# The search for the expert thresholds, its rounds written out and its reached values written turned

## The reference, cut to what matters

```python
def _L0_ffn_ref(x, gate_w, w1, w2):                 # x is (B=4, T=1024, C=256), after attention and layer norm
    cap = int(EXPERT_CAPACITY * T / E)              # E = 8 experts, cap = 256
    probs = jax.nn.softmax(jnp.einsum('BTC,CE->BTE', x, gate_w), axis=-1)
    top_p, top_idx = jax.lax.top_k(jnp.transpose(probs, (0, 2, 1)), cap)
    xin = jnp.take_along_axis(x[:, None, :, :], top_idx[..., None], axis=2)
    h = jax.nn.gelu(jnp.einsum('BElC,ECH->BElH', xin, w1), approximate=False)
    y = jnp.einsum('BElH,EHC->BElC', h, w2) * top_p[..., None]
    return jnp.zeros((B, T, C), x.dtype).at[b_idx, top_idx].add(y)
```

## Time and profile before

| what | value |
|---|---|
| median of 3 runs | 505.44 us (503.3 to 505.83) |
| the profiled execution | 505.29 us, span 503.6 us |
| PE busy | 460.6 us (91% of the span) |
| DVE busy | 309.9 us (62%) |
| ACT busy, POOL busy | 211.5 us, 189.0 us |
| the search (65.17 to 99.3 us of the span) | 34.1 us |
| mean granted TensorE clock | 0.941 of full |

### The profile page before, as it was taken

The page is one execution under the profiler, slowest core; times in us unless marked ns, Lnnn a source line. Parts: engine busy times, 40 slices in busy tenths (PEclk is TensorE's granted clock), DMA queues, the critical chain, the costliest instruction groups (busy, mean ns, idle before and its releaser), DMA issues.

```text
span 503.6 us, 9489 instructions
## 1 busy us (share of the span) xinstructions
PE 460.6 (91%) x3204; PEld 412.2 (82%) x3204; DVE 309.9 (62%) x825; ACT 211.5 (42%) x517; POOL 189.0 (38%) x175
## 2 busy tenths in 40 slices
PE   6999455568999999999999999999999999999992
PEld 5888344467999899989998999899989989999992
DVE  3787788877457545754665475557555664665450
ACT  1568498002244425524442354245424533452331
POOL 3322400051083518143722554174518252813332
PEclk9999655569999999999999999999999999999998
DMA  8963844023242615171517243433525171503131
GB/s 291 360 217 124 294 172 173 1 53 110 93 76 55 171 48 85 32 208 34 83 16 203 53 75 78 130 66 62 149 59 85 43 208 27 79 22 43 21 43 21
DMA packets 35666, 52.44 MB, mean 104 GB/s; under 512 B 3009, under 2 KB 28994, under 8 KB 35138
## 3 DMA queue, kind: packets, MB, share of 16 engines
q1 hardware_dynamic: 22400, 34.37, 20.5%
q0 software_dynamic: 12288, 17.08, 19.6%
q10 hardware_dynamic: 962, 0.80, 0.5%
HBM read 35.17 MB, written 16.92 MB: 103 GB/s over the span
## 4 chain that ended last, share of the span: by engine, by line
PE 77%; DVE 8%; issue 1%; POOL 1%; ACT 0%; DVEq 0%; POOLq 0%
PE wide L865 36%; PE bank L856 35%; PE bank L698 3%; DVE over L1124 2%; DVE floor L1137 1%; PE bank L831 1%; DVE cand L1119 1%; DVE reached L1131 1%; PE bank L815 1%; PE bank L902 1%; PE wide L698 1%; POOL out_dram L491 1%; PE bank L865 1%; DVE w1lo L1289 1%; DVE x_all L1024 0%
## 5 line engine op out<-in xcount | busy, mean ns | idle before, releaser
L865 PE MATMUL wide<-w2hi,hhi 128*128 128x256 f32 x504 | 145.4, 289 | 0.0
L491 POOL DMA_INDIRECT out_dram<-ysb,sidx x64 | 102.2, 1596 | 111.5 <-ACT ysb L651 95.1
L865 PE MATMUL wide<-w2hi,hlo 128*128 128x256 f32 x504 | 142.5, 283 | 0.0
L865 PE MATMUL wide<-w2lo,hhi 128*128 128x256 f32 x504 | 142.1, 282 | 0.0
L638 ACT ACTIVATE hraw<-bank 128x512 f32<-128x512 f32 (+1 forms) x136 | 77.6, 571 | 127.7 <-PE bank L856 124.6
L483 POOL DMA_INDIRECT xg<-xn_rows,gidx x64 | 65.2, 1018 | 156.8 <-issue 89.4
L1281 DVE CAST hhi<-hraw 128x512 fp32r<-128x512 f32 (+1 forms) x136 | 57.9, 426 | 86.9 <-ACT hraw L638 82.3
L865 PEld LDWEIGHTS wide<-w2hi,hhi 128*128 128x128 f32 x504 | 95.3, 189 | 3.7
L865 PEld LDWEIGHTS wide<-w2lo,hhi 128*128 128x128 f32 x504 | 95.1, 189 | 3.4
L865 PEld LDWEIGHTS wide<-w2hi,hlo 128*128 128x128 f32 x504 | 94.9, 188 | 0.0
L1283 DVE TENSOR_TENSOR hlo<-hraw,hhi 128x512 fp32r<-128x512 f32 (+1 forms) x136 | 90.4, 665 | 4.7
(11 more groups left out here) (175 smaller groups left out, 466.4 us busy)
## 6 DMA issues: line engine op xcount, KB each, us to landing
raw<-in_w_dram SPq DMA_DIRECT2D x16, 1024.0 KB
xn_rows<-x_all SPq DMA_DIRECT2D x4, 1060.0 KB, 4.0
raw<-in_x_turned_dram SPq DMA_DIRECT2D x8, 512.0 KB, 8.7
x_all<-in_x_dram SPq DMA_DIRECT2D x8, 512.0 KB, 9.7
out_dram<-x_all SPq DMA_DIRECT2D x8, 512.0 KB, 3.4
xg<-xn_rows,gidx POOLq DMA_INDIRECT x64
out_dram<-ysb,sidx POOLq DMA_INDIRECT x64
ctxT<-in_ctx_turned_dram ACTq DMA_DIRECT2D x1, 256.0 KB, 3.4
```

The source lines that it names most:

```text
L491: pool.indirect_dma_start(out=out_rows, out_offset=at, in_=ysb[g][:, i, :], in_offset=None, compute_op=ALU.add).then_inc(rows_added, 16)
L865: t = pe.matmul(y_tile(g, i, last), hh[s % 4][:, at:at + P], w[:, j, :], start=(j == 0 and m == 0 and (alone or i % 2 == 0)), stop=(j == H ...
```

## The change

The DVE loop over the rounds is gone: the four rounds that it held stand one after another, with the round as a constant. `reached` has the order batch, expert, bits: `keep_reached` writes each value 8 places (16 bytes) behind the one before, and `raise_floor` reads 8 in a row. `cand` and the counts have the order bits, batch, expert within a half, so `keep_reached` reads both in a row of 128; `compare` now reads `cand` in seven pieces of 8 that lie 16 values apart, and the matmul writes its 56 sums to seven pieces of 8 in PSUM.

```diff
-        cand = sb("cand", [P, B, KT + 1, E], I16)
+        cand = sb("cand", [P, 2, KT + 1, HB, E], I16)
...
-        reached = sb("reached", [P, B, KT + 1, E], I16)
+        reached = sb("reached", [P, B, E, KT + 1], I16)
...
-            return bank[h][:, 0:HB * (KT + 1) * E].rearrange("p (b n) -> p b n", b=HB)
+            return bank[h][:, 0:HB * (KT + 1) * E].rearrange("p (k b e) -> p k b e", b=HB, e=E)
...
-                            t = pe.matmul(counts(h)[:, b, E:], onesb[:], over[:, h * HB + b, c, :],
+                            t = pe.matmul(counts(h)[:, 1:, b], onesb[:], over[:, h * HB + b, c, :].rearrange("p (k e) -> p k e", e=E),
...
-                full = [P, HB, KT + 1, E]
-                dve.tensor_tensor(half(cand, h), half(floor_, h).unsqueeze(2).to_broadcast(full),
-                                  step_bits[:, bass.ds(r, 1)].to_broadcast(full), ALU.bitwise_or).then_inc(cand_ready[h], 1)
+                full = [P, KT + 1, HB, E]
+                steps = step_bits[:, r] if isinstance(r, int) else step_bits[:, bass.ds(r, 1)].rearrange("p r k e -> p (r k) e")
+                dve.tensor_tensor(cand[:, h], half(floor_, h).unsqueeze(1).to_broadcast(full),
+                                  steps.unsqueeze(2).to_broadcast(full), ALU.bitwise_or).then_inc(cand_ready[h], 1)
...
-                    half(cand, h)[:, b, 1:].unsqueeze(1).to_broadcast([P, TC, KT, E]), ALU.is_ge).then_inc(over_ready[h][b], 1)
+                    cand[:, h, 1:, b].unsqueeze(1).to_broadcast([P, TC, KT, E]), ALU.is_ge).then_inc(over_ready[h][b], 1)
...
-                dve.scalar_tensor_tensor(out=half(reached, h).rearrange("p b k e -> p b (k e)"), in0=counts(h),
-                                         scalar=float(CAP), in1=half(cand, h).rearrange("p b k e -> p b (k e)"),
+                dve.scalar_tensor_tensor(out=half(reached, h).rearrange("p b e k -> p k (b e)"),
+                                         in0=counts(h).rearrange("p k b e -> p k (b e)"), scalar=float(CAP),
+                                         in1=cand[:, h].rearrange("p k b e -> p k (b e)"),
                                          op0=ALU.is_ge, op1=ALU.mult).then_inc(reached_ready[h], 1)
...
-                dve.tensor_reduce(half(floor_, h), half(reached, h).rearrange("p b k e -> p b e k"), AX.X,
+                dve.tensor_reduce(half(floor_, h), half(reached, h), AX.X,
                                   ALU.max).then_inc(floor_ready[h], 1)
...
-                UR = 2
-                assert (ROUNDS - 1) % UR == 0
-                with dve.Fori(0, (ROUNDS - 1) // UR) as q:
-                    for i in range(UR):
-                        r = q * UR + i
-                        half_round(0, r, n0 + r, n0 + r)
-                        half_round(1, r, n0 + r, n0 + r + 1)
+                for r in range(ROUNDS - 1):
+                    half_round(0, r, n0 + r, n0 + r)
+                    half_round(1, r, n0 + r, n0 + r + 1)
...
-                dve.memset(counts(h)[:, :, 0:E], float(T))
+                dve.memset(counts(h)[:, 0], float(T))
```

## The result

The changed kernel takes 507.99 us (median of 6 runs, 507.62 to 508.44), the kernel before 505.02 (median of 6, 503.3 to 505.83). The medians lie 3.0 us apart. The ratio is 1.0072, with a 95% interval from 1.0047 to 1.0097, which is a cost of 3.6 us, between 2.4 and 4.9. The forecast was 504.6 with a range from 502.3 to 506.3: a small gain was forecast and the change loses, by more than the range allowed.

A forecast was written before the change was run, and what follows sets the result against it. The prediction took DVE to bound the search. Loop -1.0, reduce -1.5 and turned write +1.7 us sum to -0.8, so 505.4 - 0.8 = 504.6 us, range 502.3 to 506.3.

The forecast's parts named there:

- What bounds the search: In the two searches, DVE is the bound; what it saves per steady half round comes off the chain.
- The loop: Rounds of the search: removing register instructions at `cand` and the branches back gives -1.0 us.
- The reduce: Search's reduce, reading in a row instead of 16 bytes apart: 371 to 286 ns, 18 times, -1.5 us.
- the turning does nothing: Rival on the reduce: its 371 ns is the price of 16 short groups, not the step; 504.4 or 506.1, chance 0.08.
- `cand`, compare and matmul: Search instructions in their new layouts: compare stays at 385 ns, `cand` at 224, the matmul's pieces cost 0.
- The turned write: `keep_reached` writing values 16 bytes apart: 85 ns more, 285 to 370, 20 times, +1.7 us, bounds 0 and +3.4.
- twice the price of the read, 170 ns: Upper bound per `keep_reached` write, if a small write into a wider word costs a read and a write.
- if an instruction gets longer by d, its pitch does the same: DVE in a steady half round: overlap does not swallow an instruction's lengthening or shortening.
- the write pays twice, and the change ends a little slower: Rival on the `keep_reached` write: it costs +3.4 us, the sum is +0.9, time 506.3; chance 0.13.
- My estimate from it, 186 ns: Skill page's price for the `keep_reached` write: 128 x 1.45 = 186 ns, 3.7 us in all, time 506.6.
- The slack of PE: Steady half round: PE's counts can be there in 1.10 us, DVE returns after 1.195, leaving 0.095 us.
- the prediction's 0 for the clock: PE's slow-clock stretch behind the search: its shift taken as 0, bounded by 1.7 us in either direction.

The follow-up runs named there:

- unroll: Kernel before with only the loop over the rounds written out, all layouts as before; median 502.46 us (12 runs), ratio 0.9955.
- turn_loop: Changed kernel with the loop of before put back around its rounds; median 509.39 us (6 runs), ratio 1.0096.
- rows: Changed kernel with `reached` back in rows (order bits, batch, expert), so its write is one run of 128; median 501.81 us (12 runs), ratio 0.9959.
- turn_read: Changed kernel, but `keep_reached` writes one run of 128 and reads the counts and `cand` with steps; median 502.99 us (12 runs), ratio 0.9973.
- turn_f32: Changed kernel with `reached` in f32 instead of int16; median 500.22 us (6 runs), ratio 0.9924.
- pe_turn: Changed kernel, but the matmul writes the counts turned and `keep_reached` reads only `cand` with a step; median 504.36 us (10 runs), ratio 1.0012.
- gap: The rows kernel with 2-byte values of `reached` written 4 bytes apart; single execution 502.12 us.
- pair16: The rows kernel with `reached` in pairs side by side, 16 bytes from pair to pair, and the reduce in two instructions; single execution 501.46 us.
- turn_pad: Changed kernel with `reached` padded to 16 places for 8 values, so 2-byte values are written 32 bytes apart; single execution 509.24 us.
- solo8: The rows kernel with each 2-byte value of `reached` 8 bytes behind the one before; single execution 504.71 us.

## Why the prediction was wrong

- **What bounds the search** was right. DVE is the bound there, and the search's +4.4 us is on the chain.
- **The loop**: forecast -1.0, measured -1.2 (unroll) and -1.1 (the changed kernel against turn_loop). Right.
- **The reduce**: forecast 286 ns, measured 275. The 18 that count give 18 x 0.096 = 1.7, forecast 1.5. Right, with a gain slightly larger than forecast, and the rival "the turning does nothing" is out.
- **`cand`, compare and matmul** in their new layouts: forecast 0, measured 0 (rows). Right. The compare keeps its fast way through pieces of 8.
- **The turned write** is the step that failed: "I take the row nearest to it, the read at the same step: 85 ns". It is 440 ns. Its bound from above failed as well: "twice the price of the read, 170 ns". The term was +1.7 us with 3.4 as its limit. In the pitches it is 0.14 + 0.22 = 0.36 per half round, 20 x 0.36 = 7.2 us. With it the sum is -1.2 - 1.7 + 7.2 = +4.3, where the search shows +4.44, and rows gives 7.3 for the same term. I had priced a write by reads. turn_read shows that the price holds for reads in `reached` too (90 ns), and turn_f32 that a 4-byte write would have been near it (102 ns); the write of lone 2-byte values is what no row of before could price.
- The step **"if an instruction gets longer by d, its pitch does the same"** was wrong in part. Of 440 ns, 80 lie under the compare behind it; of turn_f32's 100 ns, 80 do. With the stepped read nothing is hidden: turn_read's 90 ns are in the pitch whole (0.30 from `reached` to compare, where rows has 0.20). And of the 360 ns that the turned write adds to a half round, 220 show only in the pitch of the compare behind it, 0.52 where it was 0.30. Why a part of the write's time is hidden was not tested.
- **The rival that came nearest** is "the write pays twice, and the change ends a little slower". Its direction was right and its price, 170 ns where 440 were measured, too low by a factor of 2.6. The Trainium skill (Vector Engine (DVE) Microarchitecture Reference, measured stream behaviour on trn2) has 2.50 to 2.51 ns per column for a destination that steps +24 words, measured on streams of 4-byte words. My estimate from it, 186 ns, agrees with the runs in direction but not in size: the 2-byte write pays 440 ns here and the 4-byte write at 32 bytes 102.
- **The slack of PE** was rightly seen. At turn_f32's half round of 1.40 us no steady wait for PE appears (1.9 us in all, in 4 waits), and in pe_turn, at the lower clock, it is used up.

What stays open is the mechanism behind the table above.

## What to carry to other kernels

Before a layout is turned so that a reader finds its values in a row, look at what the writer then does: a DVE write of lone 2-byte values 16 bytes apart costs 3.4 ns a value here, a stepped read 0.7 to 0.8. If a turn is needed, put it on the side that reads, which here cost as much as it gave (turn_read), or write 4-byte values, of whose price 80 of 100 ns lay under the next instruction. f32 for an int16 tile of 128 values made the difference between +4.4 us and -2.3 in the search. A price that no row shows should get bounds wide enough for a cost of another kind, and one short run of that instruction is worth more than an analogy.

## What the runs showed of the hardware that was not expected

The stretch behind the search, the same work in all kernels, differs by up to 1.8 us. The span less the start of `last_bits` is 404.6 (before), 404.7 (after) and 404.5 (unroll), but 403.0 in turn_f32 and 402.9 in rows. The granted clock has a part in it. Before, it is at 0.50 up to 106.1, full for 3.4 us and at 0.50 again from 109.5 to 112.9; in turn_f32 it rises later behind `last_bits`, and then stays full. First the kernel before, then turn_f32 (length, PE, PEld, DVE, ACT, POOL, clock, DMA, GB/s):

```profile
98.98:106.10 7.12, 3.72 (x24) 3.64 (x25) 5.58 (x23) 0.00 (x0) 1.07 (x1) 0.50 0.01 3
```

```profile
94.63:103.80 9.17, 5.26 (x30) 4.78 (x30) 7.58 (x28) 0.00 (x0) 2.50 (x3) 0.50 0.06 17
104.00:110.00 6.00, 4.61 (x37) 4.06 (x37) 3.43 (x9) 1.32 (x4) 4.78 (x5) 1.00 0.38 100
110.00:120.00 10.00, 10.00 (x65) 8.95 (x66) 9.04 (x22) 3.20 (x7) 1.31 (x2) 1.00 0.43 139
```

At 1.2 GHz, the lower level, PE was busy for 3.72 + 3.40 = 7.12 us before and for 5.26 in turn_f32. Half of the difference is 0.9 us, an estimate of what the clock can give back, where the tails lie 1.65 apart; the rest is open. Over all thirteen profiles the tails are not two values but spread from 402.9 to 404.7. In the five shortest (up to 403.2: turn_loop, turn_f32, rows, gap, pair16) the clock rises 8 to 9 us behind `last_bits` and stays full. In the others it falls again, or rises only after 13 us (turn_pad, solo8). Between the kernel before and the changed one the tails are 0.1 us apart, so the prediction's 0 for the clock came out; over the experiments the spread is 1.8 us, its bound was 1.7.

The clock also answered to the search itself: in pe_turn alone it rose there, as the rows of that kernel show.

Ahead of the search the profiles fall into two groups, though that stage is the same work in all: the first `cand` starts at 63.1 to 63.6 us in the changed kernel, rows, turn_read, turn_f32, pe_turn and pair16, and at 64.9 to 65.3 in the others. The trace shows where this arises. Eight matmuls at L719 of the attention stage, in the kernel before and in the changed one:

```profile
9.11 3.75 PE L719 MATMUL wide<-kT,wq_sb 128*128 128x256 f32 x8
```

```profile
9.53 1.97 PE L719 MATMUL wide<-kT,wq_sb 128*128 128x256 f32 x8
```

They take 3.75 us in each of the seven profiles that start the search late and 1.96 to 1.99 in each of the six that start it early. In the late ones DVE then waits once for PE at L1009, for 1.4 to 1.8 us, and in the early ones it does not. The granted clock reads 1.00 over these matmuls in the profile before as well as in the changed kernel's, so that column doesn't tell the two apart, and why PE took twice as long stays open. None of this belongs to the change. It is why two single spans can differ by more than 3 us here without the change, and why the search's own length is the better measure.
